# First node stage of a graph network: values kept in the accumulators, statistics of two steps at once, both scalings on ScalarE

## The reference, cut to what matters

```
feat_neigh = segment_sum(edge_val * feat[col], row)          # done by the stage before
h   = relu(feat_neigh @ W_neigh.T + b_neigh)
n   = (h - mean(h)) * scale * rsqrt(var(h) + 1e-9)           # + offset
x1  = layernorm(x + self_branch + offset + n)                # eps 1e-5
z   = x1 @ W1                                               # 128 -> 32, input of the next layer's sums
```

## Time and profile before

| | us |
|---|---|
| median of three runs | 14823.09 (14818.71 to 14823.97) |
| the profiled execution | 14869.26 |
| its span | 14866.8 |
| the changed stage, first turn on PE to last z | 5842.35 to 6036.35, 194.0 |

### The profile page before, as it was taken

How to read it: one execution, slowest core, us unless ns; L and a number is a source line. 1 busy time by engine, 2 the same in 40 slices (tenths; PEclk the granted TensorE clock), 3 DMA queues, 4 the chain that set the end, 5 groups by cost and what they waited for, 6 DMA issues and landing times. The chain is left out here.

```text
span 14866.8 us, 237609 instructions
## 1 busy us (share of the span) xinstructions
PE 7619.2 (51%) x49340; PEld 5813.8 (39%) x49341; DVE 9378.0 (63%) x37882; ACT 4396.3 (30%) x12927; POOL 6945.3 (47%) x7131
## 2 busy tenths in 40 slices
PE   4000000013433334899989998777777763343433
PEld 4000000003423333544454444677777753333333
DVE  6655455454434444999989998566666655555556
ACT  1000000000000001788868887444544440000001
POOL 3645545566666664000000000566666656666665
PEclk5555555555555555899989999899999985555555
DMA  4433333383211112333323333333333432222222
GB/s 110 151 100 105 103 97 106 102 116 53 46 45 46 46 45 58 86 99 99 98 69 98 98 98 86 104 106 106 106 105 105 106 89 67 68 68 68 68 68 69
DMA packets 1501997, 1286.19 MB, mean 87 GB/s; under 512 B 419162, under 2 KB 1364861, under 8 KB 1501213
## 3 DMA queue, kind: packets, MB, share of 16 engines
q1 hardware_dynamic: 1044628, 690.15, 19.2%
q0 software_dynamic: 224352, 469.74, 11.9%
q10 hardware_dynamic: 232626, 122.48, 3.1%
HBM read 1121.05 MB, written 160.62 MB: 86 GB/s over the span
## 5 line engine op out<-in xcount | busy, mean ns | idle before, releaser
L900 POOL DMA_INDIRECT work<-q_tab,pay_a x1760 | 1773.1, 1007 | 2646.0 <-DMA q_tab<-work 1691.3
L1441 PE MATMUL ps<-work 128*96 128x512 bf16 x9024 | 2628.7, 382 | 0.0
L1822 DVE TENSOR_TENSOR big<-big,ps 128x128 f32 (+1 forms) x5280 | 1499.8, 284 | 1456.6 <-issue 993.4
L867 POOL DMA_INDIRECT edges_a<-work,big x1660 | 1685.4, 1015 | 1337.2 <-DMA work<-in_edge_attr_dram 706.1
L2091 DVE TENSOR_SCALAR work<-work 128x512 bf16<-128x512 f16 x7896 | 2285.4, 356 | 3.4 <-PE ps L1441 3.2
L900 POOL DMA_INDIRECT work<-h_tab,pay_a x1760 | 1677.9, 953 | 931.1 <-issue 485.1
L900 POOL DMA_INDIRECT work<-in_x_dram,pay_a x1760 | 1686.1, 958 | 857.7 <-issue 501.1
L1437 PE MATMUL ps<-big,work 128*128 x9024 | 1876.8, 208 | 274.6 <-issue 162.8
L1311 PE MATMUL ps<-work 128*128 128x128 f32 x3520 | 911.6, 436 | 1562.3 <-DVE work L1814 639.9
L1591 PE MATMUL ps<-work 128*128 128x129 f32 x3520 | 915.9, 441 | 1128.1 <-DVE work L1814 493.1
L2041 DVE TENSOR_SCALAR work<-work,iota_p 128x512 f32<-128x512 bf16 (+1 forms) x880 | 379.1, 431 | 1759.4 <-remote 1681.9
(11 more groups left out here) (378 smaller groups left out, 15551.1 us busy)
## 6 DMA issues: line engine op xcount, KB each, us to landing
work<-pair_lo SPq DMA_DIRECT2D x2256, 128.0 KB
work<-edges_a SPq DMA_DIRECT2D x440, 256.0 KB
work<-lo_rows SPq DMA_DIRECT2D x880, 128.0 KB
pay_a<-key_rows SPq DMA_DIRECT2D x166, 640.0 KB
work<-in_edge_attr_dram ACTq DMA_DIRECT2D x166, 640.0 KB
work<-in_x_dram,pay_a POOLq DMA_INDIRECT x1760
work<-q_tab,pay_a POOLq DMA_INDIRECT x1760
work<-h_tab,pay_a POOLq DMA_INDIRECT x1760
```

The lines of the kernel that those rows point to most:

```text
L867: pool.indirect_dma_start(out=edges_a, out_offset=bass.IndirectOffsetOnAxis(ap=pos_a[:, s % POS, j:j + 1], axis=0), in_=stage_a[:, k, j, : ...
L900: pool.indirect_dma_start(out=ring[:, at:at + width], out_offset=None, in_=table, in_offset=bass.IndirectOffsetOnAxis(ap=pay[:, e, 1:2], a ...
L1441: m = pe.matmul(ps[0:H3, 4 + kk // QUADS_G, :], lhsT=pair_msg[:, kk % 4, j * H3:(j + 1) * H3], rhs=pair_hot[:, kk % 4, j, :], start=kk % Q ...
L1822: dve.tensor_tensor(o, o, tile_sums, ALU.add).then_inc(p.acc, 1)
```

## The change

1. `hid0` and `xn0` are gone. ACT writes relu into `acc` at the step's own place, and all that follows works there in place: norm a, multiply, add, statistics, norm b, the store of SP and the turn of PE.
2. The statistics are taken for BATCH[b] at a time: step 0 alone, then the pairs (1, 2), (3, 4) ... (11, 12), then step 13 alone; 8 batches in place of 14 steps, for a and for b. A batch's statistics a wait for relu of its last step.
3. The second scaling is done by ACT too, by scale and bias as the first one (`first_norm` with `mom_b`); DVE only makes the bias (`scale_of`).
4. ACT's order in iteration i is now: feat copy of i, proj copy of i-5, relu of i, z of i-5, root b (odd i), norm a of i-2, norm b of i-4, root a (even i), and the other work as before. PE's order is the same as before, with steps i and i-5 in place of i+1 and i-2. The loops have 19 iterations; before they had 18 on ACT and 17 on PE.
5. The loads have six buffers in place of three; a store follows six steps behind its load in SP's loop, before it was four. The two stores of the other work stand at s = 10 in place of s = 7.

The diff, cut to its core:

```diff
-        pre0 = take((3, BSTEP, D))
+        pre0 = take((6, BSTEP, D))
-        hid0 = take((3, BSTEP, D))
-        xn0 = take((3, BSTEP, D))
...
-            return bank_slot((i - 3) % 2)[:, 2 * BANK:3 * BANK]
+            return bank_slot(i % 2)[:, 2 * BANK:3 * BANK]
...
+            for s in range(NSTEPS + 6):
                 if s < NSTEPS:
+                    if s >= 6:
+                        sp.wait_ge(n0.var_b, BATCH_OF[s - 6] + 1)
+                    wait(sp, n0.xl[s % 3], s // 3 * 16)
+                    sp.dma_start(pre0[:, s % 6], blocks_of(pre_tab, s)).then_inc(n0.xl[s % 3], 16)
+                g = s - 6
+                if g >= 0:
+                    sp.wait_ge(n0.xnew, g + 1)
+                    sp.dma_start(blocks_of(x1_tab, g), acc_b[:, g * BSTEP:(g + 1) * BSTEP, :]).then_inc(n0.st[g % 3], 16)
...
+            def first_norm(s, m, rdy):
+                b, at = BATCH_OF[s], (s - BATCH[BATCH_OF[s]][0]) * BSTEP
+                act.wait_ge(rdy, b + 1)
+                for j in range(BSTEP):
+                    v = acc_b[:, s * BSTEP + j, :]
+                    ins = act.activation(v, v, ACT.Identity, scale=m[b % 2][7][:, at + j:at + j + 1], bias=m[b % 2][1][:, at + j:at + j + 1])
+                return ins
...
+            for i in range(NSTEPS + 5):
+                g = i - 5
...
+                    act.activation(proj0[:, g % 2], bank_slot(g % 2)[:, 2 * BANK:2 * BANK + BSTEP * D], ACT.Copy).then_inc(n0.ptrc, 1)
+                if i < NSTEPS:
+                    act.wait_ge(n0.hmm, i + 1)
+                    act.activation(acc[:, i * (BSTEP * D):(i + 1) * (BSTEP * D)], bank_slot(i % 2)[:, 0:BSTEP * D], ACT.Relu).then_inc(n0.relu, 1)
...
+                if i % 2 == 1 and 0 <= i // 2 - 1 < len(BATCH):
+                    first_root(i // 2 - 1, mom_b, n0.var_b, n0.std_b)
+                if 0 <= i - 2 < NSTEPS:
+                    first_norm(i - 2, mom_a, n0.rdy).then_inc(n0.nrm, 1)
+                if 0 <= i - 4 < NSTEPS:
+                    first_norm(i - 4, mom_b, n0.rdy_b).then_inc(n0.xnew, 1)
+                if i % 2 == 0 and i // 2 < len(BATCH):
+                    first_root(i // 2, mom_a, n0.var_a, n0.std_a)
                 if 0 <= i - 5 < BATCHES:
                     for b in range(4 * (i - 5), 4 * (i - 4)):
                         away_from_span(b)
                 if 0 <= i - 6 < BATCHES:
                     keep_columns(i)
...
+            for b in range(len(BATCH) + 1):
+                if b < len(BATCH):
+                    dve.wait_ge(n0.relu, BATCH[b][1])
+                    moments_of(b, stats0[0], mom_a[b % 2], 1e-9).then_inc(n0.var_a, 1)
+                if b >= 1:
+                    for s in range(*BATCH[b - 1]):
+                        xn = acc_b[:, s * BSTEP:(s + 1) * BSTEP, :]
+                        dve.wait_ge(n0.nrm, s + 1)
+                        c(dve.tensor_tensor(xn, xn, scale0[:, D:2 * D].unsqueeze(1).to_broadcast([P, BSTEP, D]), ALU.mult))
+                        dve.wait_ge(n0.xl[s % 3], (s // 3 + 1) * 16)
+                        c(dve.tensor_tensor(xn, xn, pre0[:, s % 6], ALU.add))
+                    if b >= 3:
+                        dve.wait_ge(n0.xnew, BATCH[b - 3][1])
+                    moments_of(b - 1, stats0[1], mom_b[(b - 1) % 2], 1e-5).then_inc(n0.var_b, 1)
+                if b < len(BATCH):
+                    scale_of(b, mom_a[b % 2], n0.std_a, n0.rdy)
+                if b >= 1:
+                    scale_of(b - 1, mom_b[(b - 1) % 2], n0.std_b, n0.rdy_b)
```

More of the change, by code:

```diff
@@ L509, in gnn_program @@
         take = carver(work, 0)
-        pre0 = take((3, BSTEP, D))
+        pre0 = take((6, BSTEP, D))
         feat0 = take((2, BSTEP * D))
-        hid0 = take((3, BSTEP, D))
-        xn0 = take((3, BSTEP, D))
         proj0 = take((2, BSTEP * D))
-        stats0 = [take((BSTEP, 6)) for _ in range(2)]
-        mom_a = [[take((BSTEP,)) for _ in range(8)] for _ in range(2)]
-        mom_b = [[take((BSTEP,)) for _ in range(8)] for _ in range(2)]
+        stats0 = [take((2 * BSTEP, 6)) for _ in range(2)]
+        mom_a = [[take((2 * BSTEP,)) for _ in range(8)] for _ in range(2)]
+        mom_b = [[take((2 * BSTEP,)) for _ in range(8)] for _ in range(2)]
         take = carver(work, 0)
@@ L765, in _ @@
             sp.wait_ge(own.stored, 16)
-            for s in range(NSTEPS + 4):
+            for s in range(NSTEPS + 6):
                 if s < NSTEPS:
[L768 to L773, removed]
+                    if s >= 6:
[6 more added lines that the diff above has]
+                    sp.dma_start(blocks_of(x1_tab, g), acc_b[:, g * BSTEP:(g + 1) * BSTEP, :]).then_inc(n0.st[g % 3], 16)
+                if s == 10:
                     sp.wait_ge(pairs.got, 16 * QB)
@@ L1006, in keep_columns @@
                 act.activation(pair_dst[:, (i - 6) * BANK:(i - 5) * BANK], turn_bank(i), ACT.Copy).then_inc(pairs.cols, 1)
[L1008 to L1027, removed]
@@ L1366, in _ @@
             pe.wait_ge(p0.acc, TILES)
[L1367 to L1371, removed]
+            for i in range(NSTEPS + 5):
+                g = i - 5
+                front = bank_slot(i % 2)
+                if i < NSTEPS:
+                    wait(pe, n0.relu, i - 1)
                     for j in range(BSTEP):
-                        at = (s * BSTEP + j) * D
-                        m = pe.transpose(front[:, j * D:(j + 1) * D], acc[:, at:at + D], ident[:, :])
+                        m = pe.transpose(front[:, j * D:(j + 1) * D], acc_b[:, i * BSTEP + j, :], ident[:, :])
                     m.then_inc(n0.tr, 1)
-                if 0 <= g < NSTEPS:
+                if g >= 0:
                     turned = bank_slot(g % 2)[:, 2 * BANK:4 * BANK]
@@ L1396, in _ @@
                     pe.wait_ge(pairs.rel, 4 * (i - 5))
-                    pe.wait_ge(n0.pev, i - 2)
+                    pe.wait_ge(n0.pev, i - 5)
                     for j in range(4):
@@ new lines, in moments_of, with scale_of @@
+            def moments_of(b, st, m, eps):
+                first, last = BATCH[b]
+                count = (last - first) * BSTEP
+                for j in range(count):
+                    ins = dve.bn_stats(st[:, j, :], acc_b[:, first * BSTEP + j, :])
+                c(ins)
+                return mean_var(c, st[:, 0:count, :], [v[:, 0:count] for v in m], eps)
+            def scale_of(b, m, std, rdy):
+                count = (BATCH[b][1] - BATCH[b][0]) * BSTEP
+                v = [u[:, 0:count] for u in m]
+                dve.wait_ge(std, b + 1)
+                c(dve.reciprocal(v[7], v[6]))
+                dve.scalar_tensor_tensor(out=v[1], in0=v[4], scalar=-1.0, in1=v[7], op0=ALU.mult, op1=ALU.mult).then_inc(rdy, 1)
```

60 lines of the change are left out of this document (17 added, 43 removed).

## The result

The changed kernel takes 14846.0 us (median of 15 runs, 14827.6 to 14856.3), the kernel before on the same chip 14818.7 (15 runs, 14784.7 to 14842.6). The ratio is 1.0018, 95% interval 1.0010 to 1.0025: slower by some 27 us, with 15 to 37 inside the interval. The forecast was 14847.9, and by the prediction's own measure, 0.2%, a ratio of 1.0018 still counts as the same. That the two totals lie 2 us apart is luck: the prediction started from a median of 14823.1, and 15 runs gave 14818.7. The test is the stage and its parts.

A forecast was written before the change was run, and what follows sets the result against it. A chain of engines taking turns, none full, was taken to bound the stage: 44.5 + 12.4 + 112.3 + 49.6 = 218.8 us against 194.0, so 14823.1 + 24.8 = 14847.9 us. Its own range was 14836 to 14860, the overall one 14822 to 14868.

The forecast's parts named there:

- The chain: From one x1 to the next, PE and ACT take turns: 8.53 and 7.51 us, 16.04 before the clock's saving.
- the fill: From the stage's start to the first turn of an x1: 44.5 us, 28.9 before.
- the drain: Last steps, no features left and PE at half clock, to the end of z: 49.6 us together.
- The middle step: Steps i = 6 to 13: 14.04 us each, after 2.0 us saved by full clock; 112.3 us for eight.
- the step without other work: Step i = 5, without ACT's additions and bank copy on the chain: 12.4 us.
- the other work on the chain: ACT's additions and bank copy, now behind norm b, ahead of PE's turn of x1: 8 x 1.75 = 14 us.
- The edits without a price: Six buffers, longer batches, in-place work and moved stores were claimed to add no time to the stage.
- Load off the fuller engine: Rival: DVE's lost load decides; stage 52 us shorter, 14771 us in all; 4 in 100.
- The clock stays up: Rival: PE keeps full clock through its unbroken stretch; step 11.8, stage 182, total 14811 us; 5 in 100.
- The clock doesn't come: Rival: PE at half clock throughout; stage 238.3 us, 44 more, total 14867; 13 in 100.
- The order costs less: Rival: additions and bank copy stay beside PE's wait; 14 us less, total 14834; 10 in 100.
- The signs: Profile checks; wrong if steps under 12.7 us, DVE on the chain past the fill, or a DMA releasing a wait.

The follow-up runs named there:

- e3: Changed kernel with only ACT's order rewritten, norm b ahead of the bank copy and norm a after it; stage 193.5 us against 216.7.
- e2: Changed kernel with the second scaling given back to DVE, the rest of the change kept; stage 189.8 us.
- e1: Changed kernel with the four small ACT additions moved from behind norm b to ahead of relu; stage 214.3 us against 216.7.
- e7: Changed kernel with three load buffers in place of six; stage 216.1 us.
- e10: Changed kernel with statistics taken by step in place of batches of two, its order kept; stage 218.2 us.
- e6: Kernel before with relu and all later values kept in the accumulators, no hid0 and xn0, nothing else changed; stage 188.7 us.
- e9: Changed kernel with 54 extra identity turns on PE (20 in the last iterations) ahead of its wait for x1; stage 198.2 us.
- e8: Changed kernel with statistics by step, second scaling on DVE ahead of its use, ACT reordered; stage 157.3 us, ratio 0.9967 to the kernel before.
- e4: Changed kernel with 40 extra identity turns on PE (20 in the last iterations) ahead of its wait for x1; stage 205.8 us.

## Why the prediction was right, point by point

- **The chain.** Right as it was told: PE waits for the bank copy, z for PE, the scalings for z. e3 shows that the order is the cause (23 us back with the same work), e2 that it acts through the second scaling (27 us). Counted by the turns of the first, second and tenth x1, before and after, the 24.0 us are 14.6 in the fill, 0.2 in the step behind it, 11.9 in the eight steps, and 2.7 less in the drain: more than half of the loss is the longer way of the first x1.
- **The middle step.** Forecast 14.04 us, measured 14.01 in the mean of the eight, from 15.2 down to 13.7. The prediction took one saving of the clock for all, 2.0 us of 8.53, with 1.5 to 2.7 as bounds. In fact PE's part went from 7.6 us to 6.0, a saving of 0.9 in the first of the eight, which is outside of these bounds, and of 2.5 in the last, 2.15 in the mean. ACT's part was 7.63 in place of 7.51. That the two errors nearly cancel in the mean is luck. The eight steps and the step without other work came to 112.1 and 13.0 us; 112.3 and 12.4 were the terms.
- **The fill** was 43.45 (44.5 forecast), **the drain** 49.5 (49.6).
- **The attribution failed.** "Of them 8 x 1.75 = 14 are the other work on the chain" treats the clock's saving as fixed. e1 took 1.17 of these 1.75 us off the chain, by that sum 8 x 1.17 = 9.4 us, and 2.4 arrived: the clock's rise came later by as much. The sum was right for the kernel as it stood, not as a price list of its parts. Its two named parts, 14 and 15.6, are already more than the 24.8 that they were to explain; what the change wins on the chain and in the drain was left unnamed.
- **The edits without a price.** Six buffers: confirmed (e7). Batches: confirmed for the middle steps of this order (e10), false for a better one, where ACT waits for them (e3). In place: no cost in one profile (e6).
- **DVE's second scaling** was priced at 2.80 us and is 1.89 by itself (last section). This left the forecast alone, as the piece was read from the chain with its neighbour in it. Nor does it explain e2's miss, since the chain doesn't wait for these scalings in the middle there.
- **The rivals.** Load off the fuller engine: DVE lost 48 us of busy time and the stage grew by 24. The clock stays up: 0.52 at the turn and 0.72 from the turn to z, where it asked for about 0.9; its step, 11.8, is near what e9 made (12.05), its stage of 182 isn't (198.2). The argument against it, that PE starts at 0.50 after each pause, had an exception already in the kernel before (0.99 us for the turn of x1 at 5960.66), and PE's pause turned out 6.4 us, not over 7. The clock doesn't come: it came in each middle step, and stayed away in the drain as taken. The order costs less: the wait of 57.8 us for L1007 refutes it.
- **The signs.** No wait in the stage ended with a DMA, and no middle step was under 12.7 us. DVE does end one wait past the fill, 0.47 us for the last bias in the drain (6014.05); the prediction names DVE on the chain as a sign against itself, yet its own sum of the drain has this wait in it. DVE was busy 90.2 us (87 forecast), ACT 134.0 (134).

## What to carry to other kernels

Engines that work in order make a ring: write down what stands between one output and the next on each of them, and price a change by what it puts into that ring, not by how full the engines are; only when one is full, as DVE in e8, does its load count. Work that a step doesn't need belongs behind a wait that is there anyway, and a value that is on the chain should be made one iteration early. Compare the stage that was changed, not the span: the spans here differed by 22 us in the wrong direction.

## What the runs showed of the hardware that was not expected

- **DVE's small scalings are slower beside GpSimd's casts and additions.** Seven of them (128x128, f32) took 1.89 us in the one step of the kernel before in which GpSimd did nothing, and 2.80 in the 13 others, where its split of z (L882 to L888) lies beside them for 1.7 us. From the timeline of the kernel before, DVE in that one step:

```profile
5869.27 1.89 DVE L1958 TENSOR_SCALAR work<-work 128x128 f32<-128x128 f32 x7
```

  and GpSimd beside the 2.80 us at 5906.73:

```profile
5906.50 0.37 POOL L882 CAST big<-big 128x224 bf16<-128x224 f32 x1 [10.61 <-ACT big L1031]
...
5908.08 0.61 POOL L888 TENSOR_TENSOR big<-big 128x224 bf16<-128x224 f32 x1
```

  In e8, where z no longer releases both at once, 12 of 14 took 1.88 to 1.89, two of these beside indirect gathers of GpSimd; the other two lay beside its split of z and took 2.38 and 2.69. In e2's fourteen, 4.57 us together, the first seven have the split beside them and take 2.78, the next seven don't and take 1.87. So 0.9 us of DVE's part in nearly each step of before was this. The Trainium skill, "SBUF — State Buffer", section "SBUF: two separate sides", says that a DVE instruction in a two-port mode and a GpSimd instruction contend for one shared pair of ports, and that the one which starts first holds it for the whole instruction. These rows fit that and give the price for this pair of operations; that it was the ports no run here shows.
- **The clock's rise does not follow the work.** Taking 1.17 us out of a step of 13.7 left it at 13.65 (e1), and turns of x1 in one stage found either level of the clock (e6). The Trainium skill, "TensorE: Matmul & The Clock Gate", section "What's actually happening", says that the point at which it comes up differs from run to run of one kernel; that would fit e6, and the two profiles of the kernel before agree as far as they go, since full clock met the eighth x1's turn in one and the sixth's in the other. No run here repeats e6.
- **With a pause of 2.1 us in PE's work the clock fell in about half of the middle steps, with one of 0.55 us in none** (e4, e9). These are two runs of this kernel, not a limit.
